# Issuing attention scores behind the transposes of the odd step, in a fused attention and mixture-of-experts layer

## What is computed

```python
xn = layernorm(x)
q, k, v = split(xn @ w_qkv)               # 16 heads of 16, window blocks of 64
scores = einsum('bhnqd,bhnkd->bhnqk', qb, k_kv) / sqrt(16)   # k_kv: block before + own block
scores = where(band_mask, scores, -1e30)
attn = softmax(scores, axis=-1)
ob = einsum('bhnqk,bhnkd->bhnqd', attn, v_kv)
out = x + merge_heads(ob) @ w_out + moe(xn)
```

## Time and profile before

| | |
|---|---|
| median of 3 runs | 763.7 us (761.96 to 763.91) |
| the profiled execution | 769.01 us, of which 767.2 us are the span from first to last instruction |
| TensorE, matmul busy | 701.0 us (91%) |
| TensorE, weight loads | 601.3 us (78%) |
| VectorE busy | 482.4 us (63%) |
| ScalarE busy | 489.7 us (64%) |
| GpSimd busy | 442.3 us (58%) |
| mean granted clock of TensorE | 0.951 of 2.4 GHz |
| attention phase | from 468 us to the end |

### The profile page before, as it was taken

How to read it: one execution, slowest core, us unless ns; L and a number is a source line. 1 busy time by engine, 2 the same in 40 slices (tenths; PEclk the granted TensorE clock), 3 DMA queues, 4 the chain that set the end, 5 groups by cost and what they waited for, 6 DMA issues and landing times. The chain is left out here.

```text
span 767.2 us, 18478 instructions
## 1 busy us (share of the span) xinstructions
PE 701.0 (91%) x5817; PEld 601.3 (78%) x5817; DVE 482.4 (63%) x1769; ACT 489.7 (64%) x1546; POOL 442.3 (58%) x846
## 2 busy tenths in 40 slices
PE   6654799999999999999999998999999999999876
PEld 3343689898898988989889897788787888788665
DVE  7962243533435334354343524899999999999993
ACT  4556470834708347093470914998989899898880
POOL 5544560543605436053360501999999999999991
PEclk9876799999999999999999997999999999999995
DMA  9633131142311423114231013132423425141321
GB/s 315 235 110 98 64 105 55 62 137 82 100 57 62 137 82 107 50 62 137 82 108 50 7 35 110 34 95 65 110 90 87 118 61 144 35 115 59 89 63 35
DMA packets 52309, 69.96 MB, mean 91 GB/s; under 512 B 6672, under 2 KB 44816, under 8 KB 52240
## 3 DMA queue, kind: packets, MB, share of 16 engines
q1 hardware_dynamic: 45744, 52.31, 21.1%
q0 software_dynamic: 6144, 16.79, 7.7%
q10 hardware_dynamic: 352, 0.04, 0.0%
HBM read 47.75 MB, written 16.78 MB: 84 GB/s over the span
## 5 line engine op out<-in xcount | busy, mean ns | idle before, releaser
L1068 ACT ACTIVATE a_p<-a_p,a_nmax 128x128 f32<-128x128 f32 x512 | 198.2, 392 | 34.2 <-DVE a_nmax L1097 34.2
L999 POOL TENSOR_SCALAR a_p<-a_p,a_rsum 128x128 f32<-128x128 f32 x512 | 192.4, 392 | 15.8 <-DVE a_rsum L1105 13.5
L733 DVE TENSOR_TENSOR m_hl<-m_hf,m_hh 128x512 fp32r<-128x512 f32 x128 | 93.3, 729 | 99.6 <-ACT m_hh L690 94.7
L55 PE MATMUL m_psY<-m_w2h,m_hh 128*128 128x256 f32 x512 | 145.2, 284 | 3.0 <-issue 3.0
L55 PE MATMUL m_psY<-m_w2h,m_hl 128*128 128x256 f32 x512 | 144.0, 281 | 1.6 <-issue 1.6
L55 PE MATMUL m_psY<-m_w2l,m_hh 128*128 128x256 f32 x512 | 143.9, 281 | 0.1
L654 POOL CAST m_w2h<-raw 128x256 fp32r<-128x256 f32 x64 | 26.1, 407 | 183.3 <-PE m_psY L55 127.3
L686 ACT ACTIVATE m_hf<-m_psF,b1T 128x512 f32<-128x512 f32 x128 | 88.3, 690 | 65.8 <-PE m_psF L55 50.7
L1097 DVE CUSTOM_DVE_ANT_0 a_p<-a_psS,mask 128x128 f32<-128x128 f32 x512 | 116.5, 280 | 5.7 <-PE a_psS L1221 5.2
L55 PE MATMUL m_psF<-m_xh,w1h 128*128 128x512 f32 x256 | 103.5, 404 | 1.5 <-DVE m_xl L710 1.5
L719 DVE TENSOR_TENSOR y<-m_psY,b2b 128x256 f32<-128x256 f32 x64 | 27.2, 424 | 120.7 <-PE m_psY L55 92.5
(11 more groups left out here) (185 smaller groups left out, 1374.9 us busy)
## 6 DMA issues: line engine op xcount, KB each, us to landing
raw<-in_L_ffn_w SPq DMA_DIRECT2D x16, 1024.0 KB, 5.0
y_scratch<-y SPq DMA_DIRECT2D x64, 128.0 KB, 1.7
n_xin<-in_L_attn_x SPq DMA_DIRECT2D x8, 512.0 KB, 7.5
xn_scratch<-n_xn SPq DMA_DIRECT2D x8, 512.0 KB, 6.6
a_res<-in_L_attn_x SPq DMA_DIRECT2D x8, 512.0 KB, 3.7
out<-a_res SPq DMA_DIRECT2D x8, 512.0 KB, 3.0
xnr<-xn_scratch SPq DMA_DIRECT2D x7, 512.0 KB, 5.0
b2b<-in_L_ffn_b SPq DMA_DIRECT2D x8, 128.0 KB, 5.1
```

Source lines behind the costliest of these rows:

```text
L55: last = pe.matmul(out, a, b, start=(n_start and i == 0), stop=(n_stop and i == n - 1))
L733: dve.tensor_tensor(hl[:, u // HC, u % HC, :], hf[:, u % FR, :], hh[:, u // HC, u % HC, :].bitcast(fp32), ALU.subtract).then_inc(hl_done, 1)
L999: pool.tensor_scalar(e, e, rsum[:, r, j:j + 1], 0.0, ALU.mult, ALU.add).then_inc(norm_done, 1)
L1068: act.activation(e, e, ACT.Exp, scale=-1.0, bias=nmax[:, r, j:j + 1], accum_out=sums[:, r, j:j + 1]).then_inc(exp_done, 1)
```

## The change

Two lines go and two come, in TensorE's list alone. The scores of steps T and T+1 (T even) are issued in the odd step T-1, right behind its transposes and ahead of its attention product and products. Before, they were issued at the end of the even step T-2. `scores` itself, its waits and their values are the same, and so is the number of calls.

```diff
@@ steps(b, ts, first, last), TensorE @@
                         for j in range(BLK):
                             ins = pe.transpose(psP[g % 2][:, j * P:(j + 1) * P], pr[:, g % PR, j, :], m.eye[:, :])
                         ins.then_inc(t_done[g % 2], 1)
+                    if t % 2 == 1 and (t < BS - 1 or t == BS - 1 and not last):
+                        scores(b, t + 1, first)
                     g = lagged(t, LAG_V, first)
                     if g is not None and g < BS and g % GRP == GRP - 1:
...
                                 product(kind, j, 1 - u, count(b, u, i, first, last), i % 2,
                                         16 * (b * 2 + u + 2), (b * 2 + u) * (STEPS // GRP), parts)
-                    if t % 2 == 0 and (t < BS - 2 or t == BS - 2 and not last):
-                        scores(b, t + 2, first)
```

## The result

| kernel | runs | median | range |
|---|---|---|---|
| before, beside it | 4 | 763.81 us | 761.96 to 764.84 |
| after | 4 | 770.63 us | 769.32 to 772.11 |

The ratio is 1.0105, with a 95% interval of 1.0070 to 1.0141: slower by 0.7 to 1.4%. The forecast was 768.9 us and +0.68%. The profiled execution of after took 769.32 us (span 767.5), almost what that of before took, which was a long one. So the spans don't show the loss; the units do.

The account below looks back on a forecast made before the run. VectorE was taken as the bound, with 0.26 us idle a unit. Losses of 0.8 us over six units (4.8) plus 0.4 at the start gave +5.2 us, +0.68%, scaled to 768.9 us; range 762.0 to 773.5.

Parts of the forecast that it names:

- The exchange: In odd steps, scores behind transposes make the attention product 0.45 us later, or 0.6 if the 0.17 us gap stays.
- GpSimd at 0: GpSimd's normalisations would not hold the transposes: cost 0, with about 0.8 us of cover.
- The reciprocal of step 8: VectorE's reciprocal waits for ScalarE, delayed through its even half at step 6: 0.35 us a unit (0 to 0.5).
- Maxima wait for scores: VectorE's maxima of step 0 would wait for later scores: 0.05 us a unit, range 0 to 0.3.
- The reciprocal of step 0: VectorE's reciprocal stalls for ScalarE, delayed through its attention output, after 0.22 us of cover: 0.3 us a unit (0.1 to 0.5).
- x copies: ScalarE's two x copies, read by VectorE with 0.1 us of cover, would cost 0.1 us a unit (0 to 0.2).
- Start and end: Attention phase start, scores of step 8 behind transposes: 0.4 us once (0 to 0.5); end, 705 to 767 us: 0.
- The loop: Copy, transposes, scores, maxima and hand-overs take 3.5 us, under VectorE's shortest pair of 3.74, so do not set the pace.
- The signs: After: VectorE idle 0.3 us before reciprocals 0 and 8, unit 35.5 us; wrong if VectorE's instruction times shift.
- Hidden after all: Rival: TensorE's lag ends in slack or in ScalarE's waits; 762 to 766 us, chance 0.27.
- TensorE is the bound: Rival: TensorE's issue order sets the pace and the gap before the attention product goes; 758 to 762 us, chance 0.13.
- The closed loop: Rival: switching and hand-overs cost 0.3 us more, so short pairs run at the loop's pace; 784 us, chance 0.05.

Follow-up runs that it names:

- experiment 2: The changed kernel with VectorE's copy put ahead of the maxima in each step; 769.19 us, ratio to before 1.0059.
- experiment 7: The changed kernel with ScalarE reading the v product behind its exp instead of ahead of it; 783.47 against 776.76 us for before, ratio 1.0094.
- experiment 1: The kernel before, its order kept, but scores of T also wait for VectorE's copy of T-7; 771.9 against 764.41 us, ratio 1.0095.
- 10: The kernel before with the attention product issued ahead of the odd step's transposes; 772.05 against 772.46 us, ratio 1.0009.
- 11: The kernel before with a wait for the copy of T-7 added only to the scores of steps 0, 4, 8, 12; 765.15 against 763.4 us, ratio 1.0016.
- 3: The kernel before with VectorE's copy put ahead of the maxima in each step, as a control; 766.76 us, ratio 1.0031.
- 9: The kernel before with transposes issued twice in steps 3 modulo 4, where no v product is read; 777.09 against 772.46 us, ratio 1.0063.
- experiment 5: Scores moved only in steps 1 modulo 4, which also issue an attention product; 784.48 against 776.76 us for before, ratio 1.0106.
- 6: Scores moved only in steps 3 modulo 4, with no attention product behind them; 777.19 against 776.76 us for before, ratio 1.0007.
- 12: The changed kernel with the attention product issued ahead of the odd step's transposes; 782.8 against 763.4 us for before, ratio 1.0229.

## Why the prediction was right

**The exchange** (lag of 0.45, "with it 0.6"): right in mechanism, too small. It measured 0.72. I let the pair start when the copy ends; it starts 0.15 later, the hand-over that I had used elsewhere and left out here. And the pair doesn't get shorter: transposes to scores cost 0.56, not 0.42, so the 0.17 us gap ahead of the product is not won.

**The waits in its place**: as named (scores' waits for maxima at most 0.2, transposes wait instead, 0.90 at step 14), though the view gives them GpSimd's name. **GpSimd at 0**: held in the units, where its normalisation ended 0.66 us ahead of the copy at step 14. The cover is real but thin: in experiment 2 the wait is for GpSimd, though at little cost.

**The reciprocal of step 8** (0.35): the distance grew by 0.25, by the route that was forecast, over ScalarE's attention output. The two numbers in it were off against each other. The lag at this product is 0.64 us (its last group starts 1.60 ahead of the reciprocal of step 6 in before, 0.96 in after), not 0.45; the cover is 0.36, not 0.1, since the output starts 0.47 behind the last group in after (621.43 to 621.90) and could have started at 620.61 in before. **Maxima wait for scores** (0.05, up to 0.3): nothing of the loss can be put to it. They do wait 0.20 to 0.32 us in the pair of step 6, but ScalarE sets its end.

**The reciprocal of step 0** (0.3): measured 0.73. Here the step of the prediction that failed is the route and its cover: it followed ScalarE's attention output with 0.22 us of cover, but the next thing that ScalarE reads is the v product, which moves by the whole lag (0.72) and had no cover (it started 0.09 us behind the reciprocal of step 14, straight behind the output in ScalarE's queue). The 0.22 was read in an untypical unit. In the one from 600.94 us the pair takes 4.36 us, and VectorE waits 0.15 us in it for a gathered expert output; in the five others it takes 4.22 and the reciprocal starts 0.10 behind ScalarE's last read, which is the hand-over and no cover. **x copies** (0.1): 0.01. The errors cover each other: 0.8 us a unit forecast, 0.93 measured; six units 4.8 against 5.56 us. That this sum is so near is luck, with the largest term at 0.3 in place of 0.73.

**Start and end** (0.4 and 0): not settled. By the ratio the total is 1.0105 x 763.8 - 763.8 = 8.0 us, interval 5.3 to 10.8, so the forecast of 5.2 us lies just under its lower edge. The units explain 5.56 of it. The first part is 2.02 us longer, and 1.66 of that stands between the reciprocals of steps 4 and 6 (4.85 us at clock 0.83, 6.51 at 0.67): TensorE runs at 1.2 GHz from about 1.7 to 12.0 us behind the start of the first scores in before, from about 1.1 to 14.7 in after. That may be part of the loss, for the kernel of experiment 7, which has the same order there, shows 6.51 at 0.67 again, and those of 1, 10 and 11, with before's order, 4.78 to 5.00 at 0.80 to 0.84. But those of 3 and 9, which don't move the scores either, show 6.46 at 0.78 and 5.95 at 0.65. There is one profiled execution of each, so it stays open; and experiment 1 has nearly the whole loss without it.

**The loop** (3.5 us under 3.74): held; the distance 12 to 14 stays 3.73.

**The signs.** VectorE idles in front of its reciprocals and the unit is 35.81 us (35.5 had been said), idle time in it 0.89 us, before 0.27. One sign of being wrong came in part: a third of the units' loss is VectorE's busy time, which grew by 1.88 us. Experiment 1 loses as much with more idle time in front of the reciprocals, so I read the longer instructions as filling a wait; no run tests it.

**The rivals.** "Hidden after all" fell by the ratio and by experiment 5, and with it the use it made of a rule of the Trainium skill (Perfetto Trace Analysis, Identifying the Most-Contended Engine): by weight-load time TensorE had 6.0 us free, yet a lag of 0.72 us cost 0.93 and 1.7 us of added work lengthened the unit by 0.73 and 0.93. Read for which engine is the fullest, the rule agreed; read as room for a delay, it didn't. "TensorE is the bound" fell as well: the gap of 0.17 us ahead of the attention product went, but one of 0.17 us came ahead of the scores, and the kernel got slower. The closed loop didn't come.

**Shown and not shown.** Shown, for the six units: the wait for the copy alone makes the loss (1); with the copy out of its way the moved scores cost 0.07 us a unit (2 against 3); the loss in 14 to 0 needs the moves ahead of an attention product (5 against 6), and goes through ScalarE's v read (7 takes the reciprocals' waits away). Not shown: what the other 2.4 us of the 8.0 are, and a version with the moved scores that is as fast as before: 2 pays for VectorE's new order, 7 and 12 met the next wait.

## What to carry to other kernels

When two groups in an in-order queue change places, ask which waits the one that goes first brings along: the second now waits for both. Price the delay by following all reads of the delayed engine's later results, not the first one; the one that counts had no cover at all. Read a cover in several units: the one unit read here had 0.22 us where the others had none. In a loop where four engines are over 90% busy, a transfer of idle time is rarely free, and a probe that adds work can change the bound: prefer one that adds only a wait.

## What the runs showed of the hardware that was not expected

Of two waits on one instruction, the trace can name the one that ended first: the row at 601.53 says GpSimd (ended 600.72), where the copy ended at 601.38. Check the ends of both.

ScalarE starts the attention output 0.47 us after the start of the product's last group of matmuls when it has been waiting for some time (603.86 to 604.33 in after), but 0.94 us after it in before (603.30 to 604.24), also while waiting. It isn't the order of issue alone: experiment 1, in before's order, shows 0.45 to 0.47 in the six units. What makes the difference wasn't tried.

Idle time in a row isn't the whole stall: with 0.73 us lost between two reciprocals, VectorE's row shows 0.40 us idle and an instruction that got longer (0.68 us in place of 0.47). Distances between the same instruction of successive steps gave the loss to 0.02 us.
